# First LayerNorm split between ScalarE and wide VectorE operations, with smaller relief of VectorE, in a one-core attention and mixing layer

## The reference

```
x2  = x + (y - mean(y)) / sqrt(var(y) + eps) * gamma + beta
z   = layernorm(x2)
xk  = z_prev + mu_k * (z - z_prev);   xr = z_prev + mu_r * (z - z_prev)
out = x2 + sigmoid(xr @ W_r) * (square(relu(xk @ W_k)) @ W_v)
```

## Time and profile before

| what | value |
|---|---|
| median of 3 timed runs | 290.34 us (289.49 to 290.89) |
| the profiled execution, its own time | 289.32 us |
| its span (first to last instruction) | 287.6 us |
| mean granted clock of TensorE | 0.982 |
| busy | PE 263.5 us (92%), DVE 239.6 (83%), ACT 151.9 (53%), POOL 130.6 (45%) |

### The profile page before, as it was taken

How to read it: one execution, slowest core, us unless ns; L and a number is a source line. 1 busy time by engine, 2 the same in 40 slices (tenths; PEclk the granted TensorE clock), 3 DMA queues, 4 the chain that set the end, 5 groups by cost and what they waited for, 6 DMA issues and landing times.

```text
span 287.6 us, 7543 instructions
## 1 busy us (share of the span) xinstructions
PE 263.5 (92%) x2961; PEld 188.9 (66%) x2961; DVE 239.6 (83%) x588; ACT 151.9 (53%) x305; POOL 130.6 (45%) x152
## 2 busy tenths in 40 slices
PE   6987988966999999999999999999999899977794
PEld 6745557634885598558875788558855776744663
DVE  6587597899699989998999899996999778988523
ACT  2385675371555864386628845685148610444540
POOL 2628522124953567445644584356435322273210
PEclk9999999995699999999999999999999999999999
DMA  6810120000200022000400020002000110002112
GB/s 167 269 45 28 49 75 2 2 1 3 73 2 2 0 81 69 1 3 24 125 2 2 3 73 2 0 3 76 1 2 2 45 32 0 1 2 73 36 36 73
DMA packets 12178, 10.73 MB, mean 37 GB/s; under 512 B 2288, under 2 KB 12144, under 8 KB 12144
## 3 DMA queue, kind: packets, MB, share of 16 engines
q1 hardware_dynamic: 11392, 9.97, 10.7%
q10 hardware_dynamic: 752, 0.30, 0.4%
HBM read 6.07 MB, written 4.19 MB: 36 GB/s over the span
## 4 chain that ended last, share of the span: by engine, by line
PE 76%; DVE 13%; issue 4%; POOL 3%; ACT 2%; DMA 1%; DVEq 0%; POOLq 0%; ACTq 0%
PE ps_x L459 10%; PE ps_x L381 8%; PE ps_z L430 6%; PE ps_x L474 6%; PE ps_x L481 6%; PE ps_y L446 5%; PE ps_y L451 5%; PE ps_x L375 5%; PE ps_z L481 4%; PE ps_x L499 4%; PE ps_x L467 3%; PE ps_z L474 3%; PE ps_x L368 2%; DVE probs L984 2%; PE ps_z L413 2%
## 5 line engine op out<-in xcount | busy, mean ns | idle before, releaser
L984 DVE TENSOR_TENSOR probs<-ps_z,causal 128x512 f32<-128x512 f32 x64 | 40.8, 679 | 4.7 <-PE ps_z L430 4.7
L459 PE MATMUL ps_x<-wo_sb,oT 128*128 128x256 f32 x128 | 29.6, 382 | 0.0
L277 POOL TENSOR_TENSOR out_tok<-tanh_r,x_tok 128x512 f32<-128x512 f32 x14 | 18.7, 1340 | 23.7 <-DVE tanh_r L1057 23.4
L254 POOL TENSOR_TENSOR xb_tok<-x_in,beta_bc 128x1024 f32<-128x1024 f32 x8 | 18.9, 2362 | 20.7 <-DVE x_tok L1030 20.7
L381 PE MATMUL ps_x<-aT,wq_sb 128*128 128x512 f32 x60 | 27.8, 605 | 0.0
L262 POOL TENSOR_TENSOR prod<-qf,ksum 128x1024 f32<-128x1024 f32 x6 | 14.1, 2355 | 29.5 <-DVE ksum L954 29.5
L459 PEld LDWEIGHTS ps_x<-wo_sb,oT 128*128 128x128 f32 x128 | 23.7, 191 | 3.8 <-issue 0.9
L217 POOL TENSOR_TENSOR rstd<-rstd,neg_half 128x4 f32<-128x4 f32 x24 | 25.1, 1045 | 1.9
L430 PE MATMUL ps_z<-qf,kfT 32*128 32x128 f32 x512 | 23.8, 300 | 1.4 <-ACT rden_bc L709 0.5
L446 PE MATMUL ps_y<-qf,state 32*32 32x128 f32 x512 | 20.9, 278 | 2.9 <-DVE oT L998 2.4
L446 PEld LDWEIGHTS ps_y<-qf,state 32*32 32x32 f32 x512 | 12.1, 105 | 17.1 <-issue 11.8
(11 more groups left out here) (143 smaller groups left out, 606.9 us busy)
## 6 DMA issues: line engine op xcount, KB each, us to landing
x_in<-in_L_attn_x_dram SPq DMA_DIRECT2D x8, 512.0 KB, 4.3
out_dram<-out_tok SPq DMA_DIRECT2D x16, 256.0 KB, 2.1
xr<-in_L_attn_Wq_dram ACTq DMA_DIRECT2D x1, 256.0 KB, 4.2
xk<-in_L_ffn_W_r_dram SPq DMA_DIRECT2D x1, 256.0 KB, 5.5
xk<-in_L_ffn_W_k_dram SPq DMA_DIRECT2D x1, 256.0 KB, 5.7
xr<-in_L_ffn_W_v_dram SPq DMA_DIRECT2D x1, 256.0 KB, 6.3
wo_sb<-in_L_attn_Wo_dram SPq DMA_DIRECT2D x4, 64.0 KB, 4.9
bo_bc<-in_L_attn_bo_dram SPq DMA_DIRECT2D x1, 128.0 KB, 5.5
```

What stands on the lines that cost most here:

```text
L254: PL.tensor_tensor(xb_tok[n % 2][:], x_in[n % XBUF][:], beta_bc[:].unsqueeze(1).to_broadcast([P, NB, D]), ALU.add).then_inc(s_xb, 1)
L459: last = mm(bk_[:, (b % 2) * D:(b % 2 + 1) * D], oT[m % 2][:, a, b, :], wo_sb[:, a, :], start=(a == 0), stop=(a == 1))
L984: V.tensor_tensor(probs[b % 2][:, 2 * h:2 * h + 2, :].rearrange("p g (r s) -> p g r s", s=HALF), ps_z[:, 2 * h:2 * h + 2, 0:2 * P].rearran ...
```

## The change

- First LayerNorm: POOL's `first_norm` now makes a scale and a bias (four small operations instead of two). ACT's new `normalise_y` writes (y - mean) * rstd in place in four operations of 128x256. DVE's `times_gamma` multiplies by gamma in two operations of 128x512, and `second_residual` adds x + beta in two of 128x512. The eight operations of DVE with a scalar per partition are gone.
- Keys: DVE writes one copy of the key features `kf` and ACT copies it (`double_keys`) where it wrote two; PE's transposes of the keys wait for that copy.
- Masks: one operation of 128x1024 in place of two of 128x512, released when all scores are there.
- Order: in the like steps the shifts for xk move ahead on DVE, and POOL adds bo before the first norm. In step 1 `prod` is made by DVE instead of POOL. In the finale DVE makes x2 and its statistics of chunk 6 before the shifts for xr of chunk 5, POOL makes the second norm of chunk 7 before it finishes chunk 5, and ACT writes z of chunk 7 before both gates of chunk 6.

The diff, with unchanged lines cut to the nearest ones:

```diff
@@ -100,9 +100,12 @@
                       for name, shape in (("ka", (2, T)), ("wv", (KD, D))))
+        s_kd = sem("kf_doubled")
         s_kah, s_kal, wv_split = sem("kact_high"), sem("kact_low"), sem("wv_split")
...
         stats1, mv1, rstd1 = sb("stats1", NB, 6), sb("mv1", NB, 2), sb("rstd1", NB)
+        neg_mean1, nbias1 = sb("neg_mean1", NB), sb("nbias1", NB)
+        s_nb1, s_n1, s_g1 = sem("nbias1_ready"), sem("y_scaled"), sem("y_gamma")
         stats2, mv2, rstd2, neg_mean2, nbias2 = sb("stats2", NB, 6), sb("mv2", NB, 2), sb("rstd2", NB), sb("neg_mean2", NB), sb("nbias2", NB)
@@ -230,10 +233,9 @@
             def first_norm(m):
-                pool.wait_ge(s_st1, 8 * m + 8)
                 if m >= 1:
-                    pool.wait_ge(s_x2, 4 * m)
-                rstd(rstd1, mv1, s_rs1, 2 * m + 1)
+                    pool.wait_ge(s_n1, 4 * m)
+                scale_and_bias(m, mv1, neg_mean1, rstd1, nbias1, s_st1, s_rs1, s_nb1)
@@ -283,16 +285,15 @@
                     norm_x(n + 1)
-                if m >= 0:
+                if f >= 0:
+                    add_bo(n)
                     first_norm(m)
-                if f >= 0:
-                    add_bo(n)
                     add_beta(n)
...
                     if m >= 0:
-                        denominator_terms(n)
+                        first_norm(m)
                         second_norm(m)
@@ -311,8 +312,8 @@
                 token_difference(m)
+                second_norm(c)
                 finish(f)
-                second_norm(c)
                 finish(m)
@@ -383,6 +384,8 @@
                 pe.wait_ge(s_kf, 2 * n + 2)
+                if n >= 1:
+                    pe.wait_ge(s_kd, n)
                 for b in range(NB):
@@ -740,6 +743,10 @@
+            def double_keys(n):
+                act.wait_ge(s_kf, 2 * n + 2)
+                copy(kf[:, :, :, 1, :], kf[:, :, :, 0, :]).then_inc(s_kd, 1)
+
             def state_blocks(n):
@@ -770,6 +777,12 @@
                                   scale=rstd0[:, b:b + 1]).then_inc(s_a, 1)
+
+            def normalise_y(m):
+                act.wait_ge(s_nb1, 2 * m + 2)
+                for b in range(NB):
+                    AC.activation(y_tok[:, b, :], y_tok[:, b, :], ACT.Identity, bias=nbias1[:, b:b + 1],
+                                  scale=rstd1[:, b:b + 1]).then_inc(s_n1, 1)
@@ -820,11 +833,16 @@
                     gate_r(f, 0, x1)
+                double_keys(n)
+                if f >= 0:
+                    normalise_y(m)
                     gate_r(f, 1, x2)
...
                 state_blocks(n)
+                if m >= 0 and f < 0:
+                    normalise_y(m)
                 if c == 0:
@@ -847,16 +865,18 @@
                 shift_z(f, x0, x1)
+                normalise_y(m)
                 channel_k(f, 0, z0)
...
                 shift_z(m, x0, x2)
+                normalise_y(c)
                 channel_k(m, 0, z0)
                 channel_k(m, 1, z1)
+                normalise_z(c)
                 gate_r(m, 0, z2)
-                normalise_z(c)
                 gate_r(m, 1, z3)
@@ -935,10 +955,10 @@
                 dve.wait_ge(s_ekm, n + 1)
-                for j in range(2):
+                for j in range(1 if n else 2):
                     V.scalar_tensor_tensor(out=kf[:, :, :, j, :], in0=kb[:].rearrange("p b (g d) -> p b g d", d=HD),
                                            scalar=1.0, in1=ek[:].rearrange("p b (g d) -> p b g d", d=HD),
-                                           op0=ALU.add, op1=ALU.max).then_inc(s_kf, 1)
+                                           op0=ALU.add, op1=ALU.max).then_inc(s_kf, 2 if n else 1)
@@ -979,12 +999,11 @@
                     dve.wait_ge(s_o, 4 * c + b - 1)
-                for h in range(2):
-                    dve.wait_ge(s_sc, 8 * c + 2 * b + h + 1)
-                    V.tensor_tensor(probs[b % 2][:, 2 * h:2 * h + 2, :].rearrange("p g (r s) -> p g r s", s=HALF),
-                                    ps_z[:, 2 * h:2 * h + 2, 0:2 * P].rearrange("p g (r s) -> p g r s", s=HALF),
-                                    causal[:].unsqueeze(1).unsqueeze(1).to_broadcast([P, 2, 4, HALF]),
-                                    ALU.mult).then_inc(s_pr, 1)
+                dve.wait_ge(s_sc, 8 * c + 2 * b + 2)
+                V.tensor_tensor(probs[b % 2][:].rearrange("p g (r s) -> p g r s", s=HALF),
+                                ps_z[:, :, 0:2 * P].rearrange("p g (r s) -> p g r s", s=HALF),
+                                causal[:].unsqueeze(1).unsqueeze(1).to_broadcast([P, G, 4, HALF]),
+                                ALU.mult).then_inc(s_pr, 2)
@@ -1004,7 +1023,7 @@
                         dve.wait_ge(s_x2, 4 * m)
-                        dve.wait_ge(s_rs1, 2 * m)
+                        dve.wait_ge(s_n1, 4 * m)
                 dve.wait_ge(s_y_ps, 2 * m + i + 1)
@@ -1013,22 +1032,21 @@
-            def centre(m):
-                dve.wait_ge(s_st1, 8 * m + 8)
-                for b in range(NB):
-                    V.scalar_tensor_tensor(out=y_tok[:, b, :], in0=y_tok[:, b, :], scalar=mv1[:, b, 0:1], in1=gamma_bc[:],
-                                           op0=ALU.subtract, op1=ALU.mult).then_inc(s_t, 1)
+            def times_gamma(m):
+                for i in range(2):
+                    dve.wait_ge(s_n1, 4 * m + 2 * i + 2)
+                    part = y_tok[:, 2 * i:2 * i + 2, :]
+                    V.tensor_tensor(part, part, gamma_bc[:].unsqueeze(1).to_broadcast([P, 2, D]), ALU.mult).then_inc(s_g1, 1)
             def second_residual(m):
-                dve.wait_ge(s_rs1, 2 * m + 2)
                 dve.wait_ge(s_xb, m + 1)
...
                     dve.wait_ge(s_z, 4 * m - 8)
-                for b in range(NB):
-                    dve.wait_ge(s_t, 4 * m + b + 1)
-                    V.scalar_tensor_tensor(out=x2_tok[m % 3][:, b, :], in0=y_tok[:, b, :], scalar=rstd1[:, b:b + 1],
-                                           in1=xb_tok[m % 2][:, b, :], op0=ALU.mult, op1=ALU.add).then_inc(s_x2, 1)
+                for i in range(2):
+                    dve.wait_ge(s_g1, 2 * m + i + 1)
+                    V.tensor_tensor(x2_tok[m % 3][:, 2 * i:2 * i + 2, :], y_tok[:, 2 * i:2 * i + 2, :],
+                                    xb_tok[m % 2][:, 2 * i:2 * i + 2, :], ALU.add).then_inc(s_x2, 2)
@@ -1073,14 +1091,14 @@
                 keys_values(n)
-                centre(m)
                 key_features(n)
-                second_residual(m)
+                token_shift(f, 0, *for_k)
+                token_shift(f, 1, *for_k)
                 divide(c, 0)
                 mask(c, 2)
+                times_gamma(m)
+                second_residual(m)
                 queries(n, 0, x0)
-                token_shift(f, 0, *for_k)
-                token_shift(f, 1, *for_k)
                 queries(n, 1, x1)
@@ -1111,16 +1129,14 @@
                 queries(n, 0, x0)
-                if m >= 0:
-                    centre(m)
                 queries(n, 1, x1)
...
                 key_sums(n)
-                if m < 0:
-                    denominator_terms(n)
+                denominator_terms(n)
                 mask(c, 3)
                 if m >= 0:
+                    times_gamma(m)
                     second_residual(m)
@@ -1142,18 +1158,18 @@
                 divide(c, 3)
-                centre(m)
+                times_gamma(m)
+                second_residual(m)
+                second_stats(m)
                 token_shift(f, 0, *for_r)
                 token_shift(f, 1, *for_r)
-                second_residual(m)
-                second_stats(m)
                 add_residual(c, 0, x2)
                 add_residual(c, 1, x0)
-                centre(c)
                 gate(f, 0, x1)
...
                 token_shift(m, 1, *for_k)
+                times_gamma(c)
                 second_residual(c)
```

1 line of the change is left out of this document (removed).

## The result

The changed kernel takes 296.86 us (median of 4 runs, 296.13 to 297.80) where the kernel before takes 290.05 (4 runs beside it, 289.49 to 290.89): ratio 1.0239, interval 1.0206 to 1.0272, 6.8 us slower. The forecast was 291.6 with a range from 288.9 to 294.2. In the table of the experiments the ratios of kernels 2 and 3 are lower than their medians suggest, since runs far above a kernel's fastest are left out of a ratio. The profiled execution took 297.23 us, with a span of 295.5 against 287.6, and a mean granted clock of 0.960 against 0.982.

The account below looks back on a forecast made before the run. PE was taken to bound the kernel, with DVE only keeping up in like steps. Masks -0.5, step 1 +0.25 and finale +1.5 gave +1.25 us: median 290.34 becomes 291.6, range 288.9 to 294.2.

Parts of the forecast that it names:

- the finale's term of +1.5 us: Finale: 2.2 for PE's wait, -1.25 for DVE's shifts and 0.6 for a gate, together +1.5 us.
- the clock falls in the finale too: Rival, finale: the clock falls with PE's waits before `mix_r` and the last `mix_k`; net +3.6 us or more, 294; chance 0.13.
- The price of 2.4 us: Cost of one clock fall, read from PE's work in step 1: 5.12 us against 2.76 in a like step.
- the masks: All steps: single masks end 0.06 us sooner each, counted 8 or 9 times where PE waits; -0.5 us.
- the stall: Finale: xr of chunk 5 stands behind x2 and statistics of chunk 6, so PE starts `mix_r` at 249.8; +2.2 us.
- the shifts without `finish` beside them: Finale: DVE from xk of chunk 6 to the statistics of chunk 7 takes 5.1 us instead of 6.32; -1.25 us.
- the gate ahead of the transposes: Finale, ACT: one more gate stands between z of chunk 7 and the copies of its transposes; +0.6 us.
- nothing: Bound on the masks' gain: none, since the single operation must also wait for the last scores.
- Step 1: Step 1: the third divide on DVE starts at 66.79 instead of 66.55, and z of chunk 0 follows; +0.25 us.
- The first rival: Step 1: the clock does not fall, 2.4 us come back; net -1.1 us, 289.2; chance 0.14.
- The like steps: Like steps: PE stays full, DVE's relief gains nothing, and ACT's added work is costed at 0.
- its sum of 2.76 us for four wide operations: Step 1, DVE: the skill's fixed cost charged in full to four wide operations; the forecast kept 2.40 instead.

Follow-up runs that it names:

- kernel 2: The changed kernel with ACT's and POOL's finale orders of before (first gate ahead of z, `finish` ahead of the second norm): 296.01 us, ratio 1.0119.
- kernel 3: The changed kernel with the masks as pairs of 128x512, each behind its own wait for scores: 295.94 us, ratio 1.0122.
- kernel 1: The changed kernel with the finale's shifts for xr of chunk 5 again ahead of x2 and statistics of chunk 6 on DVE: 291.62 us, ratio 1.0046.
- kernel 12: The changed kernel with the finale's shifts for xr first again and the masks in pairs: 290.76 us, ratio 1.0028.
- Experiment 11: The kernel before with single masks of 128x1024, timed: 290.02 us, ratio 1.0013.
- experiment 6: The kernel before with unused identity matmuls in PE's waits of steps 0 and 1: 289.47 us, ratio 0.9990.
- experiment 7: The changed kernel with the finale's xr shifts first and unused identity matmuls in steps 0, 1 and ahead of the last `mix_k`: 288.64 us, ratio 0.9939.
- experiment 4: The changed kernel with eight unused identity matmuls ahead of `mix_r` of chunk 5 and seven ahead of the last `mix_k`: 294.53 us, ratio 1.0152.
- experiment 10: The whole change, its order kept, with unused identity matmuls in the waits of steps 0, 1 and the finale: 291.38 us, ratio 1.0057.
- experiment 9: The changed kernel with xr shifts first, identity matmuls in the waits, pair masks, and `prod` of step 1 on POOL again: 287.86 us, ratio 0.9934.

## Why the prediction was wrong

**The mechanism was named, its weight was wrong.** The failed step is that the finale's term of +1.5 us held nothing for the clock: its fall there stood only as the rival "the clock falls in the finale too", which got a chance of 0.13, argued from one fall behind waits of 2.91 and 1.07 us and a full clock at 1.51. The profiles of the change and of kernels 1, 2, 3 and 12 have seven single waits of PE of 2.16 to 2.47 us in the finale. Five were followed by a fall, two (both in kernel 3) by the full clock. Of the waits of 1.5 to 1.9 us in the finales only one was (kernel 2, behind 1.66 and 0.48 us). So at the length that I forecast for both waits, a fall at each was likelier than not, as far as seven waits of five kernels can tell. The price of 2.4 us was that of step 1, too high for one fall (1.6 and 1.7) and too low for the two that came (3.3). The Trainium skill ("TensorE: Matmul & The Clock Gate", "What's actually happening") says that the point at which the clock rises at the start of a kernel varies between runs of the same kernel. Of the falls in mid-kernel experiment 3 shows the like, with 291.8 in one run and 295.3 to 296.7 in the others.

In the profiled execution the change came out 7.9 us later where +1.25 was forecast. The 6.65 us between them are 3.3 for the two falls in the finale, 1.6 for the one in step 0, 0.6 for the finale's other terms, 0.5 for the masks, 0.75 for the last store, and -0.1 for the rest.

**Kept out of the sum: step 0.** I took its clock as full, since the change leaves that part of PE alone. It fell in the profile of the change: 1.6 of the 7.9 us. Experiment 11 gives no sign that the masks bring it, and it comes with the old order as well. The kernel before seems to pay for it too in some three runs of ten (the spans of 289 us or more), but only profiled executions show where the clock fell, so that part is argued. How often each of the four falls came in the other three runs of the change is open for the same reason; their clocks of 0.960 to 0.967 lie close to the 0.960 of the profiled one.

**The finale's terms.** Forecast +2.2 for the stall, measured +2.65. The 0.45 us are POOL's: one small operation was added ahead of the norm, and that moved the next one behind the start of DVE's xk shift (242.12). POOL's timeline of the changed kernel:

```profile
242.04 0.20 POOL L224 TENSOR_TENSOR neg_mean<-mv,neg_one 128x4 f32<-128x4 f32 x1 [3.10 <-DVE mv L935]
242.19 0.73 POOL L218 TENSOR_TENSOR rstd<-mv,ln_eps 128x4 f32<-128x4 f32 x1
243.00 1.40 POOL L220 TENSOR_TENSOR rstd<-rstd,neg_half 128x4 f32<-128x4 f32 x1
244.48 0.20 POOL L228 TENSOR_TENSOR nbias<-neg_mean,rstd 128x4 f32<-128x4 f32 x1
```

The addition (L218) took 0.73 us where such an operation takes 0.20; that DVE's shift beside it is the cause is argued from the start times and from the same line, which takes 0.71 us at 251.29 beside the xr shift and 0.20 at 255.42 with DVE idle. The expected start of y on ACT was 242.45; the measured one, 244.72 less the 1.76 us that the kernel was late by then, 242.96. Forecast -1.25 for the shifts without `finish` beside them: from xk (262.73) to the statistics (267.84) DVE takes 5.11 us instead of 6.32, -1.21, right (the prediction's own terms give 5.14, so -1.18). Forecast +0.6 for the gate ahead of the transposes: 0.65, right. The term becomes 2.1 instead of 1.5; its mechanism stood.

**The masks.** Forecast -0.5. Measured, single against pairs: at z's transposes of step 3 -0.1 us in the old kernel (104.26 in kernel 11, 104.38 before) and +0.3 in the changed one (104.74 in kernel 1, 104.47 in kernel 12), so no gain to speak of in the start, and +0.03 us a like step. The single operation is shorter (1.22 us against 1.28 for the pair), but begins later: the pair's first half began 0.65 us behind the start of the gate ahead of it (165.37 to 166.02), the single one 0.74 (167.06 to 167.80), since it waits for the last scores. That bound was named, "nothing", and should have been the value taken.

**Step 1.** Forecast +0.25, measured +0.3. The earlier start was 0.6 us (1.58 late in step 0, 1.00 here; 0.53 forecast); the stretch from the second query feature to the divide took 7.50 us (60.95 to 68.45) against 6.60, +0.90 where 0.77 was laid out. PE's waits became 1.69 and 3.13 us; forecast were 1.0 and 3.2, and the clock fell. The first rival did not come.

**The like steps.** Right: they hide the relief, the copies of the keys, y on ACT and the new order. What the prediction did not see is step 2. With the clock full at its start DVE paces it in the old kernel, which is where the changed one gains 1.2 us (experiments 6 and 7); the price of 2.4 us for step 1's fall, and with it the first rival's gain, was too high for the same reason: it is 0.6 in the kernel before.

**DVE's errata.** The Trainium skill ("VectorE: DVE Perf Modes", the section on the TRN2 errata) gives, as an estimate by its formula, 1224 ns for 1024 columns; the masks took 1212 in the mean. The choice against its sum of 2.76 us for four wide operations was right: two pairs ran from 264.11 on at 1.28 us each, with the next operation at 266.52, 2.41 us behind, and in experiment 7 from 64.85 to the divide at 67.25 in 2.40.

## What to carry to other kernels

Relief of an engine that only has to keep up gains nothing where another engine is full, so look first at what its new order does to that engine: here the place of two calls on DVE cost 2 to 2.7 us by itself, and the clock's fall behind it 1.6 more in the profile. Where a change gives TensorE a wait of some 2 us, price the wait and, at better than even odds in this kernel, a fall of the clock behind it; filling the wait with matmuls that nobody uses (experiments 4, 7 and 10) takes away what the falls cost, though not the wait, and in kernels 4 and 7 most of the scatter too (0.5 and 0.7 us between the fastest and the slowest run). In the kernel before it gained nothing that can be measured (experiment 6). Then keep the parts of a change that pay and undo the rest: experiment 9 has the split norm, the old place of xr, the old masks and filled waits, and is 0.7% faster than before; the filled waits alone give 0.1% (experiment 6), inside the interval of no change.
